# A four-layer graph network on one core: the third layer's DMA queue order, the three borders between layers, and the first layer's softmax weights

## What is computed

```python
x = _layernorm(x + _L0_gnn_ref(x, edge_index, edge_weight, edge_attr_64, ...))   # attention over edges
x = _layernorm(x + _L1_gnn_ref(x, src, dst, ...))             # mean of the sources, two linear maps, relu
x = _layernorm(x + _L2_gnn_ref(x, weight, src, dst, edge_type_8))   # 8 relations, summed over the edges
x = _layernorm(x + _L3_gnn_ref(x, ..., src, dst, edge_type_3, node_type_3))   # 3 message types, 3 node types
# in the first layer, for each edge and head:
alpha = jnp.where(alpha >= 0, alpha, 0.2 * alpha)
amax = jax.ops.segment_max(alpha, dst, num_segments=n)
ex = jnp.exp(alpha - amax[dst])
denom = jax.ops.segment_sum(ex, dst, num_segments=n)
attn = ex / (denom[dst] + 1e-16)
```

## Time and profile before

| | |
|---|---|
| median of 3 runs | 1772.02 us (1771.62 to 1773.1) |
| the profiled execution | 1771.28 us, of which 1769.5 us from first to last instruction |
| mean granted TensorE clock | 0.905 of 2.4 GHz |
| busy share | TensorE 81%, VectorE 80%, POOL 70%, ScalarE 63% |

### The profile page before, as it was taken

One profiled execution on the slowest core, in us unless ns is written; L12 is line 12 of the kernel. 1 busy time (PEld: TensorE's weight loads), 2 busy tenths in 40 slices (PEclk: granted clock), 3 DMA queues, 4 the chain that ended last, 5 costly groups with the idle time before them and its releaser, 6 DMA issues.

```text
span 1769.5 us, 22899 instructions
## 1 busy us (share of the span) xinstructions
PE 1434.3 (81%) x6078; PEld 919.2 (52%) x6078; DVE 1420.3 (80%) x3056; ACT 1111.9 (63%) x2769; POOL 1235.5 (70%) x910
## 2 busy tenths in 40 slices
PE   4788888888888487777758788788789699999995
PEld 2555555555555376666645444444445355555552
DVE  5898998999898599999977676775777577788874
ACT  1677887888787768888884555455556434443342
POOL 7888888777778787778755554544544558888874
PEclk8888888888888799999988988888889899999998
DMA  7444444534443556777652433434324433344320
GB/s 167 97 101 106 107 113 112 110 98 108 97 110 77 130 144 183 184 185 191 181 142 73 142 96 109 132 97 127 108 86 129 128 83 93 95 101 102 92 78 22
DMA packets 165797, 205.06 MB, mean 116 GB/s; under 512 B 66825, under 2 KB 97920, under 8 KB 165668
## 3 DMA queue, kind: packets, MB, share of 16 engines
q1 hardware_dynamic: 108068, 179.45, 36.5%
q0 software_dynamic: 57600, 24.15, 8.2%
HBM read 147.12 MB, written 70.80 MB: 123 GB/s over the span
## 4 chain that ended last, share of the span: by engine, by line
PE 44%; DVE 20%; ACT 18%; issue 7%; DMA 6%; POOL 4%; SPq 1%; POOLq 0%; DVEq 0%; ACTq 0%
PE po L1368 20%; PE pb L1603 7%; DMA rel<-in_etype 5%; DVE bst L754 5%; PE pt L1357 4%; ACT x L1066 4%; DVE run L829 3%; POOL slot_all L532 3%; PE pc L1477 2%; ACT so L1262 2%; ACT res L1066 2%; PE po L1363 2%; ACT do L1066 2%; ACT xt L1109 2%; ACT so L1066 2%
## 5 line engine op out<-in xcount | busy, mean ns | idle before, releaser
L532 POOL DMA_INDIRECT xs<-target_rows,slot_all x236 | 315.0, 1335 | 234.4 <-DMA xs<-source_rows 157.9
L1066 ACT ACTIVATE x<-y,nmr,rst 125x128 f32<-125x128 f32 x800 | 322.6, 484 | 100.3 <-DVE nmr L779 100.3
L1368 PE MATMUL po<-wnt,rt 128*125 128x384 f32 x800 | 299.5, 521 | 0.0
L1357 PE MATMUL pt<-ident,x 125*128 125x125 f32 x800 | 130.7, 289 | 112.4 <-issue 112.4
L1368 PEld LDWEIGHTS po<-wnt,rt 128*125 128x125 f32 x800 | 163.3, 207 | 98.2 <-issue 23.4
L964 DVE SCALAR_TENSOR_TENSOR masked<-rel,st 128x500 f32<-128x500 int32 x175 | 107.0, 671 | 121.3 <-DMA rel<-in_etype 104.1
L1368 PE MATMUL po<-wnt,run 128*125 128x384 f32 x600 | 201.5, 486 | 0.0
L539 POOL DMA_INDIRECT out_rows<-do,last_all x100 | 146.6, 1466 | 65.4 <-issue 44.7
L1357 PEld LDWEIGHTS pt<-ident,x 125*128 125x128 f32 x800 | 100.3, 153 | 149.4 <-issue 147.9
L1603 PE MATMUL pb<-masked,wr 128*128 128x500 f32 x350 | 167.7, 623 | 0.0
L1066 ACT ACTIVATE do<-yd,nmr,rst 125x128 f32<-125x128 f32 x400 | 163.7, 483 | 6.2 <-DVE nmr L779 6.2
(11 more groups left out here) (190 smaller groups left out, 3100.8 us busy)
## 6 DMA issues: line engine op xcount, KB each, us to landing
xin<-in_x SPq DMA_DIRECT2D x100, 224.0 KB
out_rows<-res SPq DMA_DIRECT2D x100, 224.0 KB
source_rows<-so SPq DMA_DIRECT2D x75, 224.0 KB
target_rows<-do SPq DMA_DIRECT2D x75, 224.0 KB
xs<-source_rows SPq DMA_DIRECT2D x59, 224.0 KB
same<-same_d SPq DMA_DIRECT2D x50, 250.0 KB, 4.6
rel<-in_etype SPq DMA_DIRECT2D x50, 250.0 KB, 4.8
xd<-target_rows SPq DMA_DIRECT2D x46, 224.0 KB
```

What stands on the lines that cost most here:

```text
L532: return nc.gpsimd.indirect_dma_start(out=to, out_offset=None, in_=table, in_offset=bass.IndirectOffsetOnAxis(ap=index, axis=0), bounds_ch ...
L1066: last = A(to[:, j, :], y[:, j, :], ACT.Identity, scale=rst[s][:, k:k + 1], bias=nmr[s][:, k:k + 1])
L1357: last = nc.tensor.transpose(tile_of(to, j), rows_[:, j, :], ident[0:R, 0:R])
L1368: last = mm(po[0:R, j * 512:j * 512 + NT * D], left(j), wnt[:, k, :, :].rearrange("k t d -> k (t d)"), start=start, stop=stop, skip_group_ ...
```

## The change

- **Third layer, SyncE.** In each iteration `sources2(c + 4)` moves from the head of the loads behind `relations2`, `targets2` and `sums2`.
- **First layer's weights.** The scan now takes the maximum after the addition, and three VectorE operations write both exponents' arguments (two more than before); ScalarE's two Relus a chunk go. The store and load of the start flags lose one element and one small DMA.
- **Borders.** ScalarE and SyncE take the last chunks' target rows ahead of the source rows; in each border, the last one or two dense steps are taken apart and laid between the first steps of the next layer. At the last border, `dense_chain(105)` stands between `targets3(0)` and `evacuate_sources(1, 3, 0)` on ScalarE.
- **POOL.** `SOONER` is 10 for 13, the other slots are gathered 3 for each chunk, and no node types in the second layer; what is left of these comes ahead of the fourth layer.

The diff, cut to its core:

```diff
-        SOONER = 13
+        SOONER = 10
...
             store_targets0(EC - 2)
             store_targets0(EC - 1)
+            store_sources0(EC - 1)
...
             for c in range(EC):
                 d = block_of(2, c)
                 if d + 3 < NC:
                     load_dense(d + 3)
-                if there(c + 4):
-                    sources2(c + 4)
                 if there(c + 2):
                     relations2(c + 2)
                 if there(c + 1):
                     targets2(c + 1)
                 if there(c + 2):
                     sums2(c + 2)
+                if there(c + 4):
+                    sources2(c + 4)
...
-                late = SOONER + 2 * (c // 3) + c % 3
-                if c % 3 < 2 and there(late):
-                    k, n = slot_ring(late)
-                    pool.wait_ge(s_slot[k], 16 * T * (n - 1))
-                    slots1(late * T, (late + 1) * T, s_slot[k])
-                elif c > EC // 2:
-                    types2(typed, typed + 2)
-                    typed += 2
+                for i in range(SOONER * T + 3 * c, min(SOONER * T + 3 * c + 3, EC * T)):
+                    k, n = slot_ring(i // T)
+                    if i % T == 0:
+                        pool.wait_ge(s_slot[k], 16 * T * (n - 1))
+                    slots1(i, i + 1, s_slot[k])
...
+            types2(typed, EC * T)
             landed(3)
...
-                step(scan(run, 0, score, aux[b][:, :], ALU.max, ALU.add))
-                V.tensor_tensor(wb, run[:, 0, 0:C], score, ALU.subtract).then_inc(q["vE"], 1)
+                step(scan(run, 0, aux[b][:, :], score, ALU.add, ALU.max))
+                step(V.tensor_tensor(wb, run[:, 0, 0:C], aux[b][:, :], ALU.add))
+                V.tensor_tensor(wa, score, run[:, 0, 1:C + 1], ALU.subtract)
+                V.tensor_tensor(wb, wb, run[:, 0, 1:C + 1], ALU.subtract).then_inc(q["vE"], 1)
...
-            for d in range(block_of(1, EC - 1), block_of(1, EC) + GAP):
+            step(V.memset(run[:, 0, C:C + 1], 0.0))
+            for d in range(block_of(1, EC - 1), block_of(1, EC) + 1):
                 only_dense(d)
...
             masks(0, range(1, REL))
+            only_dense(block_of(1, EC) + 1)
             masks(1, range(1, 1 + EARLY))
...
             message_sums(0)
+            d = NC + 2 * LAG - 1
+            step(measure(d, chain_of(d) % 2, (2, 0, 1)))
+            variances(chain_of(d) % 2, 4, 1)
+            scales(chain_of(d) % 2, 4, s_ln)
             dve.wait_ge(s_out, NC)
...
-                A(wa, wb, ACT.Relu)
-                A(wb, wb, ACT.Relu, scale=-1.0).then_inc(q["eR"], 1)
...
-                A(wb, wb, ACT.Exp, scale=-1.0)
-                A(wa, wa, ACT.Exp, scale=-1.0).then_inc(q["eX"], 1)
+                A(wb, wb, ACT.Exp)
+                A(wa, wa, ACT.Exp).then_inc(q["eX"], 1)
...
-            for d in range(2 * EC, 2 * EC + GAP):
-                dense_turns(d - 2)
-                dense_products(d - 2)
+            dense_turns(2 * EC - 2)
+            dense_products(2 * EC - 2)
+            dense_turns(2 * EC - 1)
             pe.wait_ge(ph[0]["eN"], EC)
             pe.wait_ge(ph[0]["nF"], EC)
             turn_sources1(0)
             turn_targets1(0)
+            dense_products(2 * EC - 1)
...
             messages3(0)
             targets3(0)
+            dense_chain(NC + 2 * LAG - 1)
             evacuate_sources(1, 3, 0)
```

More of the change, by code:

```diff
@@ L1001, in _ @@
             scales(TAIL, 1, s_tail)
-            for d in range(block_of(2, EC - 1), NC + 2 * LAG):
+            for d in range(block_of(2, EC - 1), NC + 2 * LAG - 1):
                 only_dense(d)
+            read(NC + 2 * LAG - 1)
             def message_sums(c):
@@ L1245, in _ @@
                 normalize(do[b], yd[b], k % 2, 5).then_inc(q["nD"], 1)
-                results_of(d, k % 2, 2)
+                if there(c + 2):
+                    results_of(d, k % 2, 2)
             b, q, d = (EC - 1) % 2, ph[1], block_of(1, EC - 1)
+            k = chain_of(d - 1)
             act.wait_ge(s_tail, 2)
@@ L1251, in _ @@
             normalize(do[b], yd[b], TAIL, 2).then_inc(q["nD"], 1)
+            first_rows(d - 1, k % 2, 3)
+            act.wait_ge(q["stS"][1 - b], ((EC - 2) // 2) * ROWS)
+            normalize(so[1 - b], ys[1 - b], k % 2, 4).then_inc(q["nS"], 1)
             act.wait_ge(q["stS"][b], ((EC - 1) // 2) * ROWS)
             normalize(so[b], ys[b], TAIL, 1).then_inc(q["nS"], 1)
+            results_of(d - 1, k % 2, 2)
             dense_chain(d)
-            for d in range(block_of(1, EC), block_of(1, EC) + GAP):
-                only_dense(d)
             def source_rows2(c):
@@ L1263, in source_rows2 @@
                 last.then_inc(q["nS"], 1)
+            d = block_of(1, EC)
+            evacuate_dense(d - 2)
             evacuate_sources(0, 2, 7)
@@ L1267, in _ @@
             source_rows2(0)
+            dense_chain(d)
+            evacuate_dense(d - 1)
             act.wait_ge(ph[2]["vM"], REL - 1)
             evacuate_sources(1, 2, 7)
+            dense_chain(d + 1)
             source_rows2(1)
@@ L1298, in _ @@
             normalize(do[b], yd[b], TAIL, 0).then_inc(q["nD"], 1)
-            dense_chain(block_of(2, EC - 1))
-            for d in range(block_of(2, EC), NC + 2 * LAG):
+            results_of(d - 1, chain_of(d - 1) % 2, 1)
+            dense_chain(d)
+            for d in range(block_of(2, EC), NC + 2 * LAG - 1):
                 only_dense(d)
+            evacuate_dense(NC + 2 * LAG - 3)
             def messages3(c):
@@ L1603, in relations2 @@
                     mm(pb[:, 0:C], wr[:, r, :], masked[:, r, :] if r else st[:, :], start=r == 0, stop=r == REL - 1).then_inc(q["pM"], 1)
-            for d in range(block_of(1, EC), block_of(1, EC) + GAP):
-                dense_turns(d - 2)
-                dense_products(d - 2)
+            d = block_of(1, EC)
+            dense_turns(d - 2)
+            dense_products(d - 2)
             pe.wait_ge(ph[1]["rd"], EC)
             turns2(0)
-            relations2(0, range(REL))
+            relations2(0, range(REL // 2))
+            turn_rt(d - 1)
+            relations2(0, range(REL // 2, REL))
+            turn_xt(d - 1)
             turns2(1)
+            dense_products(d - 1)
             for c in range(EC):
```

78 lines of the change are left out of this document (39 added, 39 removed).

## The result

The changed kernel takes 1652.49 us (median of 4 runs, 1651.43 to 1653.32) for 1771.82 us of the kernel before (4 runs, 1768.39 to 1773.1): a ratio of 0.9329, 95% interval 0.9313 to 0.9345. The profiled execution took 1652.02 us, 1650.2 of it from first to last instruction, at a mean granted clock of 0.931 (0.905 before).

What follows compares the result with a forecast made beforehand. VectorE bounds the second layer; the third waits for the load of `rel` in a closed loop. 1771.3 - 106.9 + 1 - 8 - 7 + 9 = 1659.4, said as 1660 us, range 1641 to 1706.

Steps and rivals of the forecast that it cites:

- first case: Whole kernel as said, third layer at 13.0 to 14.2 us an iteration: 1660 us, range 1645 to 1680, chance 0.56.
- Third layer, -106.9: Masks no longer wait for the load of `rel`: 13.4 us an iteration for 18.4, 319.4 us for 426.3.
- the two floors: Third layer: VectorE's 13.15 us an iteration, and TensorE's and ScalarE's 13.12; 0.25 added for three loops that meet.
- First layer, +1: VectorE's two added operations nearly hidden in its waits, the Relus' removal giving a little back: -2 and +3.
- 1.36 against 1.41: First layer, us an iteration: VectorE's added operations against its waits for seeds and dense products; the addition just fits.
- rival 3: VectorE becomes the first layer's bound: half of 34 us shown gives 1677 us, all 1693; chance 0.14.
- -2 for the Relus and +3: First layer: -2 us taken for ScalarE's two removed Relus, +3 us beside it, together +1.
- First border, -8: First to second layer: 12 fewer slot gathers ahead on POOL, `ys` at 620.4 for 628.40; bounds 0 and -19.
- Second border, -7: Into the third layer: two dense steps ahead of the masks for three, scan at 940 for 947.19; bounds 0 and -10.
- Third border, +9: Into the fourth layer: second messages later behind first `st`, +6.9 us, about +2 for a falling clock; bounds 0 and +14.
- about as late behind the last scan as before: Third border: the fourth layer's first `st` waits for the gather alone, with no later start (1400.70 before).
- The signs named for the steps: No mask wait for `rel`, third-layer scans 13.4 us apart, clock at least 0.97, first layer 23.05, `ys` about 620, fourth-layer `st` gap 14.

Runs made afterwards that it cites:

- e1: Kernel before with only `sources2` moved behind the loads of relations, targets and resets in the third layer: 1663.81 us, ratio 0.9383.
- e2: Changed kernel with `sources2` moved back to the head of the third layer's loads: 1757.52 us, ratio 0.9913.
- e6: Changed kernel with one more 500-column TENSOR_TENSOR on VectorE in each iteration of the third layer: 1663.87 us.
- e7: Changed kernel with one more short matmul (two passes) on TensorE ahead of each chunk's relation products in the third layer: 1657.56 us.
- e3: Kernel before with only the first-layer part of the change (weights on VectorE, Relus gone, new start flags): 1772.41 us, ratio 1.0005.
- e5: Changed kernel with two more subtractions per chunk of the first layer on VectorE, results unused: 1675.98 us.
- e4: Changed kernel with slots for 13 chunks fetched ahead of the second layer again instead of 10: 1666.51 us.
- e11: Changed kernel with TensorE's first turn of source sums at the second border ahead of the dense products instead of behind them: 1648.33 us.
- e8: Changed kernel with 4 node-type gathers in each iteration of the third layer instead of 3: 1646.78 us, ratio 0.9283.
- e10: Kernel of e8 with the last dense step whole ahead of the fourth layer on ScalarE, VectorE and TensorE, as before the change: 1643.37 us.

## Why the prediction was right

Predicted 1660 us, measured 1652.49, inside the range of 1641 to 1706 and its first case (1645 to 1680). Against the profiled spans the change is worth -119.3 us where the sum said -111.9. Term by term:

- **Third layer, -106.9: -113.3.** The mechanism is shown by e1 and e2, both ways. The size was low by 6.4 us, nearly all that the sum missed. The step that was mis-sized is "the two floors are nearly equal, so I add 0.25 for three loops that meet: 13.4". The loops meet and add nothing: 13.12, as in the one undisturbed iteration of the earlier trace rows, and 13.15 had been worked out from VectorE's rows as well. An allowance on top of two floors that agree with an iteration that the trace really holds had no row behind it. e6 and e7 bear out both floors: TensorE has nothing to spare at 13.12, and VectorE by itself needs 13.04. The clock did what the earlier trace rows said: 0.31 us of idle and 0.70 us for the transposes, 1.00 in the stage. The Trainium skill, page TensorE: Matmul & The Clock Gate, section HAM oscillation — how this bites in real kernels, has a recurring wait for a DMA hold the clock down; the trace agrees also in the other direction, since with that wait gone the stage has the full clock (1.00, for 0.87 before and 0.87 again in e2). The DMA share was taken to rise to 0.54 with the pace and rose to 0.59 (155 GB/s for 112), but neither VectorE nor TensorE came to wait for a load.
- **First layer, +1: 0.** e3 shows it alone, and e5 shows that the cover was nearly used up, as 1.36 against 1.41 said. The addition was paid from the waits, and rival 3 (0.14) failed by a margin of 0.30 us an iteration instead of 0.05. The terms of the sum, -2 for the Relus and +3, were not measured apart.
- **First border, -8: -8.7.** The 12 gathers are the cause (e4). The old order's own spread (37.1 to 39.5) leaves the gain at 8.7 to 11.1.
- **Second border, -7: -5.0.** The miss is no larger than the old order's spread (51.0 to 53.1). e11 shows what held the border up: the turn behind the dense products, and with it ScalarE's seed and VectorE's masks. I had priced the dense step by VectorE's and ScalarE's work and had not followed TensorE, on which a low clock made the products long.
- **Third border, +9: +8.1.** That these are so close is in part luck. 1.7 of the 8.1 are the tail, of which the prediction says nothing, and the 6.4 that are left I had divided wrongly. Two rows came as written: POOL's first gather 15.87 us behind the last scan (15.6 said) and the second messages 14.95 behind the first `st` (14.8 said, though the items of that sum make 13.9, or 14.5 with the copy of `st`). The step that failed is that the first `st` comes "about as late behind the last scan as before": it came at 24.7 us for 27.2, and at 20.1 with the gathers spread (e8). So I put the whole loss on the second `st` and none on the 29 type gathers, while spreading them is worth 6.7 us of the stretch (5.7 of the medians), and undoing the split of the dense step 1.4, which cannot be told from the spread (e10).

The signs named for the steps are all there, except that the first layer's pace, 23.05 by the earlier trace rows, is 22.83 to 22.85 over its 22 steady iterations in both kernels.

## What to carry to other kernels

In a queue that issues in program order, what counts for an entry is not only when its own data are needed but who stands behind it: one entry that waited for the end of a chain held back a load that nobody needed to wait for, and one moved statement was worth 108 of the 119 us. When a loop gets faster, look again at all work that had been spread over its length by count: it now ends later against the loop's end, and what was free at the border is not. Where the trace holds one undisturbed iteration, take its time, without an allowance. And when a step is split over a border, follow each engine's next item through it: here the split gained nothing as written, and 6.4 us with one copy moved ahead of one dense step. Before a difference of 2 us at a border is read, look at how much it varies between profiles of kernels that are alike there.

## What was not expected of the hardware

VectorE reads as busy 485.85 of 500 us with no wait left in the list (e5), so that some 3% of a full engine show as idle: its free time is to be taken from the waits. POOL issues a gather of one index column every 1.57 to 1.58 us when nothing holds it (1.27 busy and 0.30), in each of these kernels, so that 12 of them are 19 us of queue; what they cost was less, 10.8 us, since 8.6 us of them fit in an idle ahead of POOL's first gather (11.19 us without them, 2.60 in e4). And when TensorE's granted clock comes back from 1.2 to 2.4 GHz differs between runs of the same queue. One and the same sequence of three TensorE items at the second border took 4.65 or 3.05 us for its last, which goes with a sum that is 2.5 us worse than its parts (1636.38 - 4.2 = 1632.2, measured 1634.7). In the tail it happened behind equal idles of 2.33 us: seven of the fourteen profiles have the eight products at 2.82 us, the others at 4.10 to 4.51.
